# Second graph pass: inverse spreads for two groups in one power of eight columns, first group's logits scaled one step later in SBUF

## What is computed

```python
x = x + _L1_gnn_ref(_layernorm(x), adj, L1_gnn_W, L1_gnn_a)     # graph attention, relu
x = x + _L1_ffn_ref(_layernorm(x), router_w, router_b, W1, b1, W2, b2)

def _layernorm(x, eps=1e-05):
    m = mean(x); v = var(x)
    return (x - m) / sqrt(v + eps)

def _L1_ffn_ref(...):            # 32 experts, each token goes to one
    logits = xf @ router_w.T + router_b
    idx = argmax(logits)
    h = relu(xf @ W1[idx] + b1[idx])
    return relu(h @ W2[idx] + b2[idx])
```

## Time and profile before

| | us |
|---|---|
| median of 3 runs (lowest, highest) | 1150.54 (1149.45, 1150.75) |
| the profiled execution, own time | 1146.29 |
| its span, first to last instruction | 1144.6 |
| PE, DVE, ACT, POOL busy, share of the span | 80%, 69%, 61%, 68% |

### The profile page before, as it was taken

The page is one execution under the profiler, slowest core; times in us unless marked ns, Lnnn a source line. Parts: engine busy times, 40 slices in busy tenths (PEclk is TensorE's granted clock), DMA queues, the critical chain, the costliest instruction groups (busy, mean ns, idle before and its releaser), DMA issues. The chain is left out here.

```text
span 1144.6 us, 27026 instructions
## 1 busy us (share of the span) xinstructions
PE 918.4 (80%) x6709; PEld 815.7 (71%) x6709; DVE 790.8 (69%) x3511; ACT 699.9 (61%) x2364; POOL 774.0 (68%) x1039
## 2 busy tenths in 40 slices
PE   5988889887379999999996599999984377656683
PEld 4777778776279999999996488888873255435463
DVE  6689999998569999999996168888887122221122
ACT  3999999896055555555554599999981143323320
POOL 4447887777728777877878017777887366666665
PEclk9999999988589999999999799999995565775655
DMA  9234432213257777878772212233312343232200
GB/s 210 64 98 146 145 102 74 62 53 112 83 162 209 204 205 206 204 201 210 200 202 74 66 38 76 76 80 87 80 40 74 82 121 94 80 87 84 66 21 37
DMA packets 144906, 129.22 MB, mean 113 GB/s; under 512 B 26522, under 2 KB 116511, under 8 KB 144755
## 3 DMA queue, kind: packets, MB, share of 16 engines
q1 hardware_dynamic: 124114, 91.94, 31.9%
q0 software_dynamic: 17760, 34.20, 8.5%
q10 hardware_dynamic: 2880, 1.35, 0.4%
HBM read 82.74 MB, written 47.48 MB: 114 GB/s over the span
## 5 line engine op out<-in xcount | busy, mean ns | idle before, releaser
L546 POOL DMA_INDIRECT xs<-staged,dst x256 | 260.7, 1018 | 76.9 <-issue 68.3
L1258 ACT ACTIVATE hT<-bank,wt 128x128 f32<-128x128 f32 x620 | 177.1, 369 | 123.1 <-PE bank L1488 86.4
L619 POOL DMA_INDIRECT out<-oq,xq x144 | 145.0, 1007 | 96.4 <-DVE oq L1157 57.4
L597 POOL DMA_INDIRECT x2d<-ob,xi x155 | 164.0, 1058 | 42.8 <-issue 28.5
L1470 PE MATMUL bank<-xnT,wt 128*128 128x128 f32 x1240 | 167.5, 279 | 11.1 <-ACT hT L1258 10.0
L1488 PE MATMUL bank<-w2s,hT 128*128 x1240 | 166.3, 277 | 0.6 <-ACT hT L1258 0.5
L1470 PEld LDWEIGHTS bank<-xnT,wt 128*128 128x128 f32 x1240 | 152.9, 194 | 13.9 <-issue 13.3
L1488 PEld LDWEIGHTS bank<-w2s,hT 128*128 128x128 f32 x1240 | 151.5, 193 | 1.5 <-issue 1.1
L1157 DVE SCALAR_TENSOR_TENSOR oq<-bank,xq 128x512 f32<-128x512 f32 x36 | 24.9, 692 | 173.5 <-remote 95.8
L1207 ACT ACTIVATE p<-bank,nm 128x128 f32<-128x128 f32 x256 | 105.0, 411 | 17.6 <-DVE nm L792 14.4
L1305 ACT ACTIVATE xnqT<-bank 128x512 f32<-128x512 f32 x36 | 21.5, 596 | 153.0 <-PE bank L1357 70.8
(11 more groups left out here) (262 smaller groups left out, 2249.5 us busy)
## 6 DMA issues: line engine op xcount, KB each, us to landing
wt<-wpd SPq DMA_DIRECT2D x155, 258.0 KB
xi<-xs SPq DMA_DIRECT2D x155, 66.0 KB
xq<-xs SPq DMA_DIRECT2D x144, 66.0 KB
xb<-x2d SPq DMA_DIRECT2D x32, 258.0 KB
xb<-in_x SPq DMA_DIRECT2D x32, 256.0 KB
wpd<-w1c SPq DMA_DIRECT2D x56, 129.0 KB
xs<-staged,dst POOLq DMA_INDIRECT x256
x2d<-ob,xi POOLq DMA_INDIRECT x155
```

What stands on the lines that cost most here:

```text
L546: pool.indirect_dma_start(out=xs[l], out_offset=bass.IndirectOffsetOnAxis(ap=dst[b % ND][:, c:c + 1], axis=0), in_=stag[s][:, q, 0:ROW], i ...
L597: pool.indirect_dma_start(out=x2d, out_offset=bass.IndirectOffsetOnAxis(ap=xi[t % NXI][:, ID:ID + 1].bitcast(U32), axis=0), in_=ob[:, t % ...
L619: pool.indirect_dma_start(out=orow, out_offset=bass.IndirectOffsetOnAxis(ap=xq[j % NXQ][:, q, ID:ID + 1].bitcast(U32), axis=0), in_=oq[j % ...
L1258: last = act.activation(hT[t % 2][:, j, :], HID[t % 2][:, j, :], ACT.Gelu, bias=wt[t % NW][:, c:c + 1])
```

## The change

For pass 1 alone, the spreads are made for a pair of groups at once: POOL at steps 2p+6 adds epsilon to eight columns, takes one power of eight columns and does two iotas (`spreads1`). `mv` has eight columns' room, `moments`, `var_eps`, `rstd` and `ids` count pairs. At the last steps, pair 14 stands at step 34 and pair 15 at step 35. DVE copies the first group's logits unscaled out of PSUM (L820 of the changed kernel) at its even step, and scales them in `lgb`, in place (L825), at the odd step, ahead of the second group's scaling (L829).

```diff
-        eps1 = sb("eps1", [P, G])
+        eps1 = sb("eps1", [P, 2 * G])
-        mv = sb("mv", [P, G, 2])
+        mv = sb("mv", [P, 2 * G, 2])
...
+            def spreads1(p):
+
+                n = NG + 2 * p
+                s = n % NS
+                after(pool, "moments", NG + 6 + p)
+                for m in (n, n + 1):
+                    pool.wait_ge(sem(f"scattered{m % NS}"), 16 * G * (m // NS))
+                after(pool, "rstd", NG + 5 + p)
+                pool.tensor_tensor(ve[:, :], mv[:, :, 1], eps1[:, :], ALU.add).then_inc(sem("var_eps"), 1)
+                after(pool, "var_eps", NG + 6 + p)
+                pool.tensor_tensor(staged[:, s:s + 2, :, RS], ve[:, :].rearrange("p (h g) -> p h g", h=2),
+                                   neghalf[:, :].rearrange("p (h g) -> p h g", h=2), ALU.pow).then_inc(sem("rstd"), 1)
+                for k in range(2):
+                    last = pool.iota(stag[s + k][:, :, ID].bitcast(I32), pattern=[[P, G]], base=T * (2 * p + k),
+                                     channel_multiplier=1)
+                last.then_inc(sem("ids"), 1)
...
-                after(pool, "ids", n)
+                after(pool, "ids", n if l == 0 else NG + g // 2)
...
-                    if (0, 5)[l] <= i < NG + 5 - 2 * l:
-                        spreads(l, i)
-                    if l == 1 and NG + 2 <= i < NG + 4:
-                        spreads(l, i + 1)
+                    if l == 0 and i < NG + 5:
+                        spreads(i)
+                    if l == 1 and (6 <= i <= NG + 2 and i % 2 == 0 or i == NG + 3):
+                        spreads1((i - 5) // 2)
...
-                after(dve, "var_eps", m + APART - 1)
+                p, half = divmod(m - NG, 2)
+                after(dve, "var_eps", NG + 5 + p)
                 for q in range(G):
-                    last = dve.bn_aggr(mv[:, q, :], st[:, q, :])
-                last.then_inc(sem("moments"), 1)
+                    last = dve.bn_aggr(mv[:, half * G + q, :], st[:, q, :])
+                if half == 1:
+                    last.then_inc(sem("moments"), 1)
...
-                after(dve, "rstd", n + APART)
                 o = (n - g) * G
+                if n >= NG and o == 0:
+                    dve.tensor_copy(lgb[:, 0:G * E], SM[:, LOGITS[1]:LOGITS[1] + G * E]).then_inc(sem("lg"), 1)
+                    return
+                if n >= NG:
+                    after(dve, "rstd", NG + 6 + (g - NG) // 2)
+                    after(dve, "lg", g)
+                    dve.tensor_tensor(ge3(lgb, k, E)[:, 0:G, :], ge3(lgb, k, E)[:, 0:G, :],
+                                      stag[g % NS][:, :, RS:RS + 1].broadcast_to([P, G, E]), ALU.mult)
+                else:
+                    after(dve, "rstd", n + APART)
```

More of the change, by code:

```diff
@@ L478, in _, with spreads @@
             pool.memset(eps1[:, :], EPS).then_inc(sem("eps"), 1)
-            def spreads(l, i):
-                n = l * NG + i
-                enters, leaves = l == 0 and i + 1 < NG, i >= 5
+            def spreads1(p):
[13 more added lines that the diff above has]
+                last.then_inc(sem("ids"), 1)
+            def spreads(i):
+                n = i
+                enters, leaves = i + 1 < NG, i >= 5
                 h = first_of_two(n + 1)
@@ L496, in spreads @@
                 own = slice(0, 2 * G) if enters and leaves else slice(h * G, (h + 1) * G) if enters else slice((1 - h) * G, (2 - h) * G)
-                e = eps[:, h, own] if l == 0 else eps1[:, :]
-                v = var[:, own] if l == 0 else mv[:, :, 1]
-                pool.tensor_tensor(ve[:, own], v, e, ALU.add).then_inc(sem("var_eps"), 1)
+                pool.tensor_tensor(ve[:, own], var[:, own], eps[:, h, own], ALU.add).then_inc(sem("var_eps"), 1)
                 after(pool, "var_eps", n + 1)
@@ L518, in _ @@
             pool.wait_ge(sem("eps"), 1)
-            spreads(0, -1)
+            spreads(-1)
             for e in range(E0):
```

## The result

The changed kernel takes 1209.94 us (median of 4, 1206.65 to 1222.23), beside 1150.12 us for the kernel before: ratio 1.0537, 95% interval 1.0498 to 1.0576. The forecast was 1152.3 us. Its 1.8 us of net loss became 60.

What follows compares the result with a forecast made beforehand. Pass 1 was taken as bound by a loop where DVE and ACT each wait once a pair, DVE's odd step on it. Loss 2.6 minus gain 0.8 gave +1.8 us on 1150.54: 1152.3 us, range 1148.7 to 1154.4.

Steps and rivals of the forecast that it cites:

- POOL, middle of the pass: POOL's queue in mid pass 1: one spread round per pair saves 1.1 us, worth nothing as POOL waits for `dst`; cost nothing.
- DVE, odd step: Extra SBUF multiplication in the loop ACT waits for: 0.20 us a pair, 13 pairs, loss 2.6 us (2.5 to 4.0).
- Free multiplication: Rival: PE or ACT gives the pace, so the extra DVE multiplication costs nothing; about 1149.3 us, chance 0.14.
- ACT's wait for `nm` grown from 0.8 to 1.0: Sign the prediction is right: in all 13 pairs of pass 1 ACT waits 1.0 us for DVE's `nm`, before 0.8.
- DVE, even step: Copy out of PSUM replaces a multiplication of the same size; 1.1 us of waiting for ACT hides any difference: 0.
- POOL, end of the pass: POOL's work after its last `dst` wait, with 1 us idle for group 31's moments: gain 0.8 us.
- wait for `mv` of 0.7 us: Sign the prediction is right: POOL newly waits about 0.7 us for the moments in the middle of pass 1.
- SP: SP's 0.70 us steps at the end of pass 1 end with POOL's stream: 0; upper end a shift of 3.2 us.
- POOL gives the pace: Rival: POOL's queue sets the 13.62 us pair, so 1.1 us a pair returns; 15 us less, about 1135.5, chance 0.08.
- SP sets the end: Rival: SP or the table sets the end of pass 1; +3.2 us, 1153.7 us, chance 0.13 including a 0.31 us multiplication.
- DVE and POOL block each other: Rival: the new 1.68 us power holds DVE's `pm` or `posoh` by a shared-port lock; +9.6 us, 1160, chance 0.05.
- what I don't see: Chance of 0.03 left for outcomes outside the named cases.

Runs made afterwards that it cites:

- e2: Kernel before, only with the first scatter of each pair in pass 1 held back so that eight indirect DMAs follow each other: 1205.05 us, ratio 1.0458.
- e5: Changed kernel plus an idle GpSimd power of eight columns between the two scatters of each pair in pass 1: 1153.94 us, ratio 1.0071.
- e6: Changed kernel plus an idle GpSimd power of four columns between the two scatters of each pair in pass 1: 1151.75 us, ratio 1.0061.
- e3: Kernel before with only VectorE's part of the change (even-step copy, odd-step multiplication in SBUF), GpSimd's queue as before: 1156.48 us, ratio 1.0054.
- e10: Kernel before, word for word, run once more: 1153.99 us beside 1152.49, ratio 1.0002.
- e9: Changed kernel with the eight-column spreads between the second and third DMA of a pair, so GpSimd sends two, then six: 1174.24 us, ratio 1.0185.

## Why the prediction was wrong, by its own steps

**The step that failed is "POOL, middle of the pass"**: "POOL saves 1.1 us a pair, and in the middle this is worth nothing", with its price "Cost: nothing". The times in it were right: the eight DMAs were forecast to take 10 us and took 742.24 to 752.52. What was wrong is that a queue with eight DMAs in a row would be the same to the others as one with two fours. The round of spreads that the change takes from between the fours was also the pause of 1.88 us that kept the others running, and its removal costs about 4 us a pair: e2 shows it without the rest of the change, e5 and e6 take it away again with pauses of 1.89 and 1.27 us.

How it adds up in the profiled execution, each counted from the first `nmax` of the pass: the last wait for `dst` comes at 258.8 us instead of 206.6, 52.2 us later. Of these 2.6 to 2.9 us are the multiplication (13 x 0.20 to 0.22), the rest the stalls and the lower clock behind them. The end of the pass adds 2.5, the way from the last scatter to the first `xq` read 1.7, the second mixture 5.4 and the start of the pass 0.3; together these are the 62.1 us of the last output.

**DVE, odd step.** Right in kind, place and size: 0.20 forecast, 0.21 us of spacing and 0.22 us of period measured, 2.6 us at the last scatter in e3. "Free multiplication" has fallen. The sign "ACT's wait for `nm` grown from 0.8 to 1.0" didn't come, since the stalls took the place of that wait.

**DVE, even step.** The copy at no cost: nothing in e3 speaks against it.

**POOL, end of the pass.** The gain of 0.8 us became a loss of 2.5: from the last wait for `dst` to the last scatter it takes 904.00 to 952.28, 48.3 us, before 45.8. The two waits for moments in it show why, 1.62 us where the forecast had none, and 3.13 where it had 1:

```profile
915.66 0.20 POOL L488 TENSOR_TENSOR ve<-mv,eps 128x8 f32<-128x8 f32 x1 [1.62 <-DVE mv L672]
...
925.91 0.20 POOL L488 TENSOR_TENSOR ve<-mv,eps 128x8 f32<-128x8 f32 x1 [3.13 <-DVE mv L672]
```

They follow runs of DMAs too. e6, whose pairs have no stall, tells when the moments come without it. Counted from the first DMA of pair 12 (855.17 in e6), the moments of groups 29 and 31 are there after 9.4 and 18.7 us in e6, after 9.3 and 17.8 before (the second from the earlier trace rows), and after 11.6 and 21.8 in the changed kernel. VectorE's rows in e6:

```profile
864.15 0.38 DVE L676 BATCH_NORM_AGGREGATE mv<-st 128x2 f32<-128x6 f32 x4
...
873.44 0.38 DVE L676 BATCH_NORM_AGGREGATE mv<-st 128x2 f32<-128x6 f32 x4
```

So at the end of the pass, too, the stall makes the moments later, by 2.2 and 3.2 us against e6. The signs on record for this part were a wait for `mv` of 0.7 us in the middle (it came as 4.3), the last scatter at 899 us (952.3) and the first `xq` read at 903 (958.0).

**SP.** The prediction saw the cause and read it as a local matter. It noted the steps of 0.70 us on SP's queue, and took it that "the slow steps end with POOL's stream". They do, 2.9 us behind its last DMA before (and here the same steps, of 0.72 us, are on TensorE). Its price of 0 was too low all the same: from the last scatter to the first `xq` read it takes 5.8 us instead of 4.1, with 5.0 in e10 as the scatter of one kernel. In the changed kernel the last to come is VectorE's table, whose instructions have "remote" waits of 1.8 to 2.5 us between 944.9 and 955.8, in the run of 20 and behind it. In e6, where this run is broken every eight DMAs, it takes 3.2 us. The question not asked was what GpSimd's stream does to the others wherever it runs as long.

**The rivals.** That the multiplication is free, that POOL gives the pace, and that SP sets the end didn't happen. "DVE and POOL block each other" named the right sign of trouble, one engine holding others, by another mechanism. The exclusive lock on which that rival rests doesn't show, and the new power doesn't hold VectorE: it runs from 739.12 to 740.80, and `pm`, which has both inputs in SBUF and starts 0.36 us after it, takes 0.29 us as before; `pos` takes 0.42:

```profile
739.48 0.29 DVE L781 SCALAR_TENSOR_TENSOR pm<-p 128x128 f32<-128x128 f32 x1 [0.72 <-ACT p L1234]
...
740.62 0.42 DVE L885 TENSOR_TENSOR pos<-bank,base 128x256 f32<-128x256 f32 x1
```

The Trainium skill, page "SBUF — State Buffer", section "SBUF: two separate sides", allows contention between engines only on the port pair that VectorE and GpSimd share, and says that TensorE and ScalarE never wait for anyone there. The stall measured here is not of that kind: TensorE and ScalarE stand as well.

**The chances.** "Slower" had 0.34, all of it within 10 us, and 0.03 stood for what I don't see. The range was built from the terms of the sum, and no term carried the change of pattern in GpSimd's queue.

**What stays open.** The mechanism inside the chip. What is shown is a dose: no stall with four in a row and 1.27 us of pause, 1.2 us with six, about 4 with eight, starting 7 to 9 us into a run. That fits something that fills while GpSimd sends and drains in a pause; no run here shows what it is. The Trainium skill, page "NOTIFIC — the notification-queue block", section "7.1 Overflow: three behaviours, one of which stalls the engine", describes such a thing for the path on which engines hand over their trace records: its inner queues hold the engines back when they are full. No run here shows whether that is it, and since every timed execution here has its span and clock on record, none tells whether an execution without any record would stall. Open too is whether the number of packets of a DMA counts, or only the DMAs: half as many rows in each was not tried. Nor was the order four DMAs, the new spreads, four DMAs, which by an estimate from e9's rows (the same work takes 11.9 us from 750.93 to 762.85, 2.34 of them for the spreads) and e3's period of 13.84 us would leave 2.3 us of pause in the middle of a pair and 1.9 behind it. Of e3's excess over its 2.6 us, and of a part of the changed kernel's 5.4 us more in the second mixture, only the size of the scatter between single executions is known.

## What to carry to other kernels

Before you merge or move small work in the queue of an engine that issues indirect DMAs, write down how many of them will now stand in a row and what pause is left between them; a saving of 1.1 us on an engine with time to spare took away a pause on which all the others lived. In the profile of the kernel before, look for "remote" and "issue" waits that begin late in a run of DMAs and end soon after it, and for one engine's rows at an even spacing much longer than their duration: they tell what a longer run will do elsewhere. Such a stall also costs where the sending engine seems to set the pace, for it comes back to that engine as a wait for the stalled ones; but a pause made of idle work takes the same time from it (41 us of waits against 38 us of idle powers in the second mixture). Look for work that has to be done anyway and put it between the DMAs.

## What the runs showed of the hardware

- A run of indirect DMAs on GpSimd, 0.96 us each and one every 1.27 us, slows the other engines from 7 to 9 us after its start to 1.4 to 1.9 us after its last DMA. In that time single instructions come at a spacing of 0.70 us (SP's queue) and 0.72 us (weight loads of 0.19 us).
- A pause of 1.27 us after four DMAs prevents it, one of 0.80 us mostly doesn't. Six in a row cost 1.2 us, eight about 4.
- The DMA engines' share in the stall was 0.12, so the transfers that the trace shows don't queue up in it.
- With 2.12 us of TensorE work in the 5 us of the stall, the granted clock fell from 1.00 to 0.50 (0.85 in these 5 us, 0.50 in the next 5); behind the stall of 1.2 us it stayed at 1.00.
- A multiplication of 128 x 128 with both operands in SBUF takes 0.21 us of VectorE when the next doesn't depend on it; out of PSUM it was 0.19.
- A GpSimd power of 1.68 us over SBUF doesn't hold a VectorE operation with two inputs in SBUF that starts under it (`pm`, 0.29 us with and without).
